# Adaptive-norm feed-forward kernel on one core: x of group 1 transposed, two x1 blocks per group made by ScalarE, one weight step moved

## The reference, cut to what matters

```
# x: (32, 64, 512), cond: (32, 256)
q  = relu(cond @ W3 + b3)                       # (32, 512)
x1 = (n * x + sum of x over the n = 64 rows of its batch) * q[:, None, :]
h0 = relu(x1 @ W2 + b2)
h  = square(relu(h0 @ ternary(W_fc).T))         # hidden width 2048
hn = h * rsqrt(mean(h * h) + eps)
out = x + hn @ ternary(W_proj).T
# ternary(w): bf16, groups of 64 columns, scale = mean |w|, clip(round(w / scale), -1, 1) * scale
```

## Time and profile before

| | |
|---|---|
| time, median of 3 runs | 314.17 us (314.13 to 314.35) |
| time of the profiled execution | 314.34 us |
| its span, first to last instruction | 312.5 us |
| outside the span | 1.84 us |
| PE busy | 306.2 us, 98% of the span |
| DVE, ACT, POOL busy | 184.5, 191.6, 102.7 us |
| granted TensorE clock | 1.000 |

### The profile page before, as it was taken

How to read it: one execution, slowest core, us unless ns; L and a number is a source line. 1 busy time by engine, 2 the same in 40 slices (tenths; PEclk the granted TensorE clock), 3 DMA queues, 4 the chain that set the end, 5 groups by cost and what they waited for, 6 DMA issues and landing times.

```text
span 312.5 us, 3806 instructions
## 1 busy us (share of the span) xinstructions
PE 306.2 (98%) x1294; PEld 233.3 (75%) x1294; DVE 184.5 (59%) x314; ACT 191.6 (61%) x282; POOL 102.7 (33%) x94
## 2 busy tenths in 40 slices
PE   7999999999999999999999999999999999999995
PEld 6664545446888778888888888888888888888883
DVE  0579999996978987843339225952222484222245
ACT  1687566689999968865445555444555545455540
POOL 1013333334533243433342431153433304343330
PEclk9999999999999999999999999999999999999999
DMA  6998474345634102230003300240000034000003
GB/s 181 362 289 262 125 222 134 81 133 137 199 101 104 34 1 37 44 57 2 0 0 136 135 0 1 106 166 0 0 2 0 0 134 136 0 0 0 2 2 135
DMA packets 31332, 27.03 MB, mean 86 GB/s; under 512 B 18736, under 2 KB 20816, under 8 KB 31312
## 3 DMA queue, kind: packets, MB, share of 16 engines
q1 hardware_dynamic: 29984, 26.25, 28.6%
q10 hardware_dynamic: 1328, 0.53, 0.7%
HBM read 18.39 MB, written 4.19 MB: 72 GB/s over the span
## 4 chain that ended last, share of the span: by engine, by line
PE 86%; ACT 8%; issue 2%; DMA 2%; DVE 1%; SPq 0%; ACTq 0%; DVEq 0%
PE ps_out L363 33%; PE ps_acc L351 31%; PE ps_acc L335 18%; PE ps_out L308 2%; ACT x_t L666 2%; DMA x_sb<-in_x_dram 2%; ACT x_t L663 2%; ACT w_scale L630 1%; ACT w_abs L624 1%; PE ps_out L324 1%; ACT w_t L638 1%; ACT w_t L643 1%; ACT w_sign L625 1%; PE ps_x L422 1%; ACT wv_sb L669 0%
## 5 line engine op out<-in xcount | busy, mean ns | idle before, releaser
L240 POOL TENSOR_TENSOR wv_sb<-wv_sb 128x512 f32<-128x512 f32 x55 | 71.9, 1306 | 119.5 <-DVE y_lo L515 116.5
L363 PE MATMUL ps_out<-w_t,y_hi 128*128 128x512 f32 x256 | 100.3, 392 | 0.3 <-DVE x_t L548 0.3
L351 PE MATMUL ps_acc<-h_hi,w_t 128*128 128x512 f32 x256 | 100.0, 391 | 0.0
L363 PE MATMUL ps_out<-w_t,y_lo 128*128 128x512 f32 x256 | 99.7, 389 | 0.0
L351 PE MATMUL ps_acc<-h_lo,w_t 128*128 128x512 f32 x256 | 99.6, 389 | 0.0
L513 DVE CAST y_hi<-x_t 128x512 fp32r<-128x512 f32 x64 | 30.5, 477 | 91.7 <-PE ps_out L363 82.0
L663 ACT ACTIVATE x_t<-ps_acc 128x512 f32<-128x512 f32 x64 | 37.9, 592 | 64.3 <-PE ps_acc L351 64.2
L335 PE MATMUL ps_acc<-x_t,wv_sb 128*128 128x512 f32 x128 | 56.3, 593 | 0.3 <-DVE x_t L500 0.3
L363 PEld LDWEIGHTS ps_out<-w_t,y_hi 128*128 128x128 f32 x256 | 48.1, 188 | 11.2 <-DVE x_t L548 0.8
L351 PEld LDWEIGHTS ps_acc<-h_hi,w_t 128*128 128x128 f32 x256 | 48.1, 188 | 10.2 <-issue 0.2
L351 PEld LDWEIGHTS ps_acc<-h_lo,w_t 128*128 128x128 f32 x256 | 48.0, 188 | 10.2 <-issue 0.2
(11 more groups left out here) (61 smaller groups left out, 161.2 us busy)
## 6 DMA issues: line engine op xcount, KB each, us to landing
x_sb<-in_x_dram SPq DMA_DIRECT2D x5, 1024.0 KB, 5.6
raw<-in_L_ffn_W_fc_dram SPq DMA_DIRECT2D x8, 512.0 KB, 7.0
raw<-in_L_ffn_W_proj_dram SPq DMA_DIRECT2D x8, 512.0 KB, 4.2
out_dram<-x_sb SPq DMA_DIRECT2D x16, 256.0 KB, 2.1
x_odd<-in_x_dram SPq DMA_DIRECT2D x2, 1024.0 KB, 7.4
x_sb<-in_x_dram SPq DMA_DIRECT2D x4, 256.0 KB, 5.7
wv_sb<-in_L_cond_W_dram SPq DMA_DIRECT2D x4, 256.0 KB, 8.1
x_t<-in_L_cond_W_dram ACTq DMA_DIRECT2D x1, 512.0 KB, 4.9
```

Source lines behind the costliest of these rows:

```text
L240: engine.tensor_tensor(acc, acc, y_sq[:, v % SQ_RING, :], ALU.add).then_inc(sq_added, 1)
L351: last = pe.matmul(ps_acc[:, (UNITS + v) % ACC_RING, :], w_t[:, j, k * P:(k + 1) * P], part[:, k, g * BANK:(g + 1) * BANK], start=(k == 0 ...
L363: last = pe.matmul(ps_out[:, t, :], part[:, v % RING, t * P:(t + 1) * P], w, start=(opens(v) and part is y_hi), stop=(closes(v) and part i ...
```

## The change

1. Group 1 is turned by PE transposes as groups 2 and 3 are, and its x1 is made as theirs. `sum_mat` is used for group 0 only (scaled by 1/64, with n taken into q: q_t is now n*q).
2. In groups 1 to 3, two of the four x1 blocks (`BY_SCALAR`: blocks 0 and 1 of group 1, 2 and 3 of groups 2 and 3) are made by ACT: DVE reduces the block and multiplies its eight sums by q (a 128x8 instruction); ACT's `spread_x` then makes the block by eight 128x64 activations, one for each batch, with a scale and a bias read per partition. DVE's order for the other two blocks stays reduce, add, multiply.
3. The first stage has steps 0 to 7 instead of 0 to 8 (unit 1 has none); step 8 goes to tile 0, steps 9 to 11 stand a tile later than before (2, 4, 6 instead of 1, 3, 5), step 12 at tile 11 instead of 7, steps 13 to 15 a tile or two later.
4. x of group 3 is loaded right behind that of group 2.
5. The matmuls for q stand behind the first quarter of group 0's sums instead of behind the second, and W_q is loaded first on ACT's queue.

```
-    STEP_AT_UNIT = {0: 0, 1: 1, 3: 2, 5: 3, 7: 4, 9: 5, 11: 6, 13: 7, 15: 8}
-    STEP_AT_TILE = {1: 9, 3: 10, 5: 11, 7: 12, 11: 13, 13: 14, 15: 15}
-    SUMS_OF_UNIT = [[0], [1], [2, 3], []]
-    KEEP_AT_TILE = {16: 14, 17: 15}
+    STEP_AT_UNIT = {0: 0, 3: 1, 5: 2, 7: 3, 9: 4, 11: 5, 13: 6, 15: 7}
+    STEP_AT_TILE = {0: 8, 2: 9, 4: 10, 6: 11, 11: 12, 13: 13, 14: 14, 16: 15}
+    SUMS_OF_UNIT = [[[], [], [0, 1, 2, 3], []], [[0], [1], [2, 3], []], [[0], [1], [2, 3], []]]
+    BY_SCALAR = [[], [0, 1], [2, 3], [2, 3]]
+    KEEP_AT_TILE = {17: 14, 18: 15}
...
                 if i == 0:
                     load_x(2)
-                if i == 2:
                     load_x(3)
...
-                if t == TT // 2:
+                if t == 1:
                     pe.wait_ge(condt_ready, 1)
...
             def scale_x(g, k):
                 dve.wait_ge(xt_done, KD * g + k + 1)
+                if g > 0:
...
+                    dve.tensor_reduce(sums, src, AX.X, ALU.add).then_inc(summed, 1)
+                    dve.wait_ge(summed, KD * (g - 1) + k + 1)
+                if k in BY_SCALAR[g]:
+                    dve.scalar_tensor_tensor(out=q_sums[:, k, :], in0=sums, scalar=1.0 / N, in1=q_of_batch,
+                                             op0=ALU.mult, op1=ALU.mult).then_inc(q_sums_ready, 1)
+                    return
                 wait(dve, h0_done, KD * (g - 1))
...
+            def spread_x(g, k):
+                act.wait_ge(q_sums_ready, x1_made(g, k)[1])
+                wait(act, h0_done, KD * (g - 1))
+                for b in range(GB):
+                    cols = slice(b * N, (b + 1) * N)
+                    last = act.activation(x1_t[:, g % RING, k, cols], ps_out[:, k, cols], ACT.Identity,
+                                          bias=q_sums[:, k, b:b + 1], scale=q_t[:, k, g * GB + b:g * GB + b + 1])
+                last.then_inc(x1_spread, 1)
...
             for u in range(UNITS):
                 if u > 0:
                     relu_h0(u - 1)
+                g, m = u // KD, u % KD
+                if g + 1 < GROUPS:
+                    for k in SUMS_OF_UNIT[g][m]:
+                        if k in BY_SCALAR[g + 1]:
+                            spread_x(g + 1, k)
                 if u in STEP_AT_UNIT:
                     step(STEP_AT_UNIT[u])
```

More of the change, by code:

```diff
@@ L306, in _, with sum_x_block @@
         def _(pe):
-            def sum_x_block(g, t, k):
-                return pe.matmul(ps_out[:, k, t * P:(t + 1) * P], x_of[g % 2][:, t, k * P:(k + 1) * P], sum_mat[:],
+            def sum_x_block(t, k):
+                return pe.matmul(ps_out[:, k, t * P:(t + 1) * P], x_sb[:, t, k * P:(k + 1) * P], sum_mat[:],
                                  start=True, stop=True)
[L311 to L317, removed]
             def turn_x(g, k):
                 pe.wait_ge(x_loaded[g % 2], 16 * ((g + 1) // 2))
-                pe.wait_ge(x1_ready, KD * (g - 1) + k + 1)
+                pe.wait_ge(*x1_made(g - 1, k))
                 for t in range(TT):
@@ L426, in _ @@
                 for k in range(KD):
-                    last = sum_x_block(0, t, k)
+                    last = sum_x_block(t, k)
                     if t == TT - 1:
@@ L431, in _ @@
             for u in range(UNITS):
[L432 to L437, removed]
+                g, m = u // KD, u % KD
+                if g + 1 < GROUPS:
+                    for k in SUMS_OF_UNIT[g][m]:
+                        turn_x(g + 1, k)
                 make_h0(u)
@@ L486, in scale_x @@
                 dve.wait_ge(xt_done, KD * g + k + 1)
+                src = ps_out[:, k, :].rearrange("p (b n) -> p b n", n=N)
+                q_of_batch = q_t[:, k, g * GB:(g + 1) * GB]
+                sums = batch_sum[:, k, :]
+                if g > 0:
+                    if g > 1:
+                        dve.wait_ge(*x1_made(g - 1, k))
+                    dve.tensor_reduce(sums, src, AX.X, ALU.add).then_inc(summed, 1)
[4 more added lines that the diff above has]
+                    return
                 wait(dve, h0_done, KD * (g - 1))
                 x1 = x1_t[:, g % RING, k, :].rearrange("p (b n) -> p b n", n=N)
[L489 to L498, removed]
+                if g > 0:
+                    dve.scalar_tensor_tensor(out=x1, in0=sums.rearrange("p (b o) -> p b o", o=1).to_broadcast([P, GB, N]),
+                                             scalar=1.0 / N, in1=src, op0=ALU.mult, op1=ALU.add).then_inc(x_added, 1)
+                    dve.wait_ge(x_added, x1_made(g, k)[1] - KD)
                     src = x1
-                dve.tensor_tensor(x1, src,
-                                  q_t[:, k, g * GB:(g + 1) * GB].rearrange("p (b o) -> p b o", o=1).to_broadcast([P, GB, N]),
+                dve.tensor_tensor(x1, src, q_of_batch.rearrange("p (b o) -> p b o", o=1).to_broadcast([P, GB, N]),
                                   ALU.mult).then_inc(x1_ready, 1)
@@ L680, in _ @@
             act.wait_ge(bias_loaded, 32)
+            act.activation(bq_n[:], bq_t[:], ACT.Copy, scale=float(N)).then_inc(bias_scaled, 1)
             act.wait_ge(q_done, 1)
+            act.wait_ge(bias_scaled, 1)
             for m in range(KD):
                 act.activation(q_t[:, m, :], ps_x[:, m * BATCHES:(m + 1) * BATCHES], ACT.Relu,
-                               bias=bq_t[:, m:m + 1]).then_inc(q_ready, 1)
+                               bias=bq_n[:, m:m + 1], scale=float(N)).then_inc(q_ready, 1)
             read_pair(0)
```

26 lines of the change are left out of this document (18 added, 8 removed).

## The result

The changed kernel takes **324.69 us** (median; 322.21 to 326.0 in four executions) against 314.19 us: a ratio of 1.0324, 95% interval 1.0251 to 1.0397. The forecast was 318.6 us with a range of 314.7 to 321.2: it is slower, as said, but by 10.5 us instead of 4.4, and outside the range. Two things need telling apart: why the profiled execution (322.21 us, span 320.4) is 7.9 us longer than that of before, and why the four executions lie 3.8 us apart where those of before agree within 0.25.

A forecast was written before the change was run, and what follows sets the result against it. TensorE, busy 98% of the span, and its waits were taken as the bound. First-stage loop + 2.0 and first eight tiles + 2.4 made + 4.4 us on 314.34; with the median 0.17 below, 318.6 us, range 314.7 to 321.2.

The forecast's parts named there:

- the loop of ACT and DVE in the first stage: First stage: ScalarE's late blocks make TensorE wait in units 12 and 14; second stage starts 2.0 us later.
- the one forecast in unit 14: First stage, unit 14: TensorE waits 0.65 us for relu_h0(11).
- TensorE's own work: First stage, group 1: transposes replace the 16 sums, 1.83 us less; with the head, 2.0 us ahead.
- the head's 0.15: Start of the kernel: a first group that ends earlier counts 0.15 us of gain.
- The price of a block: ScalarE's x1 blocks: 0.29 us per activation, 2.3 us a block, the second per-partition operand 0.085 us of it.
- the rival of cheaper blocks: First stage: at 0.20 us an activation, stage two starts 1.0 us earlier than before; total 315.6 us; chance 0.20.
- When ScalarE can begin them: First stage: ScalarE's block pairs of groups 1 to 3 can begin at about 21.9, 40.4 and 59.55 us.
- The first eight tiles: Second stage: later steps make project(1) wait 1.95 us, project(3) 0.95, project(5) and project(7) 0.2 each; net 2.4 us later.
- The rival in which the tables cost nothing: Second stage: TensorE has slack for a step one tile earlier, only the first stage's + 2.0 stays: 316.2 us; chance 0.05.
- The loads in a row: First stage: x of group 2 lands at 27.2 us, just before its need at 27.4; x of group 3 costs nothing.
- The earlier q, W_q first: Head of the kernel: the earlier q can't add much; 0.15 us of gain counted.

The follow-up runs named there:

- e2: Changed kernel with steps 8 to 11 at tiles 1, 3, 5, 7 instead of 0, 2, 4, 6: 321.76 us.
- e6: Changed kernel with W_q loaded behind b_q again on ScalarE's queue, q's matmuls still early: 322.69 us.
- e7: Changed kernel with q's matmuls behind two x blocks again, W_q still loaded first: 323.58 us.
- e12: e9 with ScalarE's blocks of groups 2 and 3 added: 321.15 us.
- e4: Changed kernel with a number as scale in ScalarE's block activations instead of a value per partition, leaving out the factor q: 322.02 us.
- e3: Changed kernel with the batch sums of ScalarE's blocks written to PSUM instead of SBUF: 324.78 us.
- e8: Kernel before with both head edits alone, W_q loaded first and q's matmuls behind the first x block: 318.41 us.
- e9: Changed kernel with the head of before, ScalarE's blocks in group 1 only, and steps 8 to 11 a tile later: 313.44 us.
- e1: Changed kernel with all x1 blocks of groups 1 to 3 made by VectorE again: 319.98 us.
- e11: Kernel before with q's matmuls behind the first x block and nothing else: 314.18 us.

## Why the prediction was wrong

The step that failed is **"the loop of ACT and DVE in the first stage", + 2.0 us**; it measured + 6.05 in the profiled execution, and 6.6 to 8.1 in e2, e6, e7 and e12, whose loops are the same code. The kind of wait was right (unit 12, its third and fourth blocks, for ScalarE); its size was not, a wait in unit 8 came with it, and the one forecast in unit 14 (0.65) didn't come. The starts in TensorE's timeline give about 6.2 us of waiting in units 8 and 12, where the view names 5.1 (it counts short, as in e12); with 1.6 us for the clock, less 1.9 that the transposes save, that is about 6.
- *TensorE's own work: right.* Group 1's transposes take 1.91 us as a row, and unit 2 starts at 20.52 instead of 22.41, 1.9 earlier (forecast 1.83 and the head's 0.15).
- *The price of a block: right.* 0.302 us from start to start against 0.29, the second operand 0.090 against 0.085. This was the number with most working in it, and it was not the one that decided: at 0.212 us (e4) the loop was still 1.0 us longer than before, with a late head in its favour, where the rival of cheaper blocks had it 1.0 shorter.
- *When ScalarE can begin them: wrong.* The blocks begin at 23.34, 42.54 and 62.34 us, forecast 21.9, 40.4 and 59.55. The first 1.4 us come from round_h0(1), 1.06 longer than its usual 0.42, and the 128x8 instruction, 0.56 longer than 0.17, both held by GpSimd (1.6 together; the rest ran 0.2 ahead of the forecast); each later turn adds the same 0.56 and 0.2 for the dearer activations. In this chain I had GpSimd in no step. Unit 8, which the prediction passes over, had a margin of 0.9 by its own times (fourth block needed at about 45.9, ScalarE done at 45.0); ScalarE was done at 47.4, so it turned into a wait of 1.24. In e3 the holds of the 128x8 instruction are gone, and about 1.7 us of the loop with them.
- *TensorE's clock: missing.* Behind the waits of unit 12 it fell to 0.50 for 3.4 us, 1.6 to 1.7 us more (for 6.8 us in e2, e6 and e7). I had priced a wait at its length.
- *The first eight tiles: right in kind, a little too large.* + 1.91 against + 2.4; project(1) and project(3) wait 0.85 and 0.74 (forecast 1.95 and 0.95), project(5) and project(7) have no named wait (forecast 0.2 each), and the wait at project(8) went as forecast. TensorE was ready for project(1) 9.8 us after the start of the stage, where I had 9.05, and split_y(1) ended 10.8 after it, where I had 11.0; so it waited less. The rival in which the tables cost nothing is refuted by e2.
- *The loads in a row: right, as far as is shown.* In the changed kernel TensorE names no wait for x of groups 2 and 3; in e7 it names one of 0.31 us, at unit 4. No run took this edit back by itself.
- *The earlier q, W_q first: wrong.* I gave this part 0.15 us of gain. In the kernel before it costs 4.0 us (e8): a later first sum and half rate behind it. In the profiled execution of the changed kernel it cost nothing. Of the other three, which left no rows, the one of 326.0 us had a mean granted clock of 0.994, as the profiled one had 0.993, so its 3.8 us are most likely the head's, as in e8, whose clock is shown as 1.00. The one of 323.46 had 0.989, and in e6 the two executions at 0.989 lie 0.9 us above the two at 0.993 and 0.994; so most of its 1.25 us is likely the longer stretch at the lower level behind unit 12. The one of 325.93 (0.989) would have both.

The whole, against e9: e12 adds 7.7 us for the blocks of groups 2 and 3; the table of steps 1.9; e9 itself stands 0.75 below before. That makes 8.9 of the 10.5 us; the 1.6 left are put down to the head and the clock, which differ from one execution to the next, and no run splits them.

## What to carry to other kernels

A new instruction on a chain is priced not only by its own duration but by what its engine is held by while it runs: look for one row of the same kind that is several times its usual length, and what ran beside it. Such a row stood in the trace of before, in VectorE's timeline (second below), and I passed over it; two of GpSimd's differences run from 64.89 to 67.52 us there:

```profile
64.89 2.63 POOL L715 TENSOR_TENSOR h_lo<-h_f,h_hi 128x512 fp32r<-128x512 f32 x2 [2.49 <-DVE h_hi L507]
```

```profile
62.22 0.21 DVE L465 TENSOR_SCALAR scale<-abs_sum 128x16 bf16<-128x16 f32 x1
...
66.31 1.24 DVE L465 TENSOR_SCALAR scale<-abs_sum 128x16 bf16<-128x16 f32 x1
```

Where a stage's bound is TensorE, let the engine that feeds it late have a margin in every unit, since a wait of TensorE can cost more than its length (here about 1.6 us more); and look at the order of the first loads, which here cost up to 4 us together with the place of 16 small matmuls. When you compare loops, ask what starts the chain that bounds them: here a load of weights, so that a later head hid in the loop.

## What the runs showed of the hardware

- Two waits close to each other in unit 12, of 2.0 to 2.6 us and 1.06 to 1.24 us, had a granted clock of 0.50 behind or between them, for 3.4 us in the changed kernel, e3 and e12 and for 6.8 us in e2, e6 and e7; waits of 1.20 and 0.52 us (e4) or 0.92 alone (e1) in the same unit did not.
- In the head matmuls ran at about half their later rate (eight sums 2.04 us instead of 1.06 to 1.13) where the granted clock is shown as 1.00. So in the first microseconds that column doesn't show it, and the durations do.
- When the full rate begins differs without a wait too: the first eight sums took 1.06 us in before's profile, but 1.61 in e11's, with the first sum at 5.3 us in both; and e9 and e12, with the same head, took 3.23 and 2.31 us for their first sixteen. Why is open.
- A second per-partition operand on a 128x64 activation costs 0.090 us from start to start (77 ns of the duration, 440 against 363).
